# A score matrix made in two halves: second moments about the first 512 tokens' mean

## The reference, cut to what matters

```python
b, n, d = x.shape                       # x: 64 * 32 tokens, layer-normed, d = 256
q = jnp.einsum('bnd,de->bne', x, w_q)   # 2048 columns of w_q
mean = jnp.mean(q, axis=(0, 1))
var = jnp.var(q, axis=(0, 1))
q = (q - mean) * jax.lax.rsqrt(var + BN_EPS) * bn_gamma + bn_beta
q = q.reshape(b, n, 2, H, KD).transpose(2, 0, 1, 3, 4)
sim = jnp.einsum('pbnhd,hkpd->pbnhk', q, keys)        # 64 keys for each of 16 heads
...                                     # top 8 of 64, twice; top 8 of 64 sums; gather, gelu, weigh, sum
```

## Time and profile before

| | |
|---|---|
| median of 3 runs | 2900.16 us (2898.94 to 2902.98) |
| the profiled execution | 2904.19 us, span 2902.3 us |
| TensorE (PE) busy | 2571.6 us, 89% |
| VectorE (DVE) busy | 2047.8 us, 71% |
| ScalarE (ACT) busy | 1447.9 us, 50% |
| GpSimd (POOL) busy | 651.5 us, 22% |
| mean granted clock of TensorE | 0.948 |

### The profile page before, as it was taken

The page is one execution under the profiler, slowest core; times in us unless marked ns, Lnnn a source line. Parts: engine busy times, 40 slices in busy tenths (PEclk is TensorE's granted clock), DMA queues, the critical chain, the costliest instruction groups (busy, mean ns, idle before and its releaser), DMA issues. The chain is left out here.

```text
span 2902.3 us, 79978 instructions
## 1 busy us (share of the span) xinstructions
PE 2571.6 (89%) x29950; PEld 1911.7 (66%) x29951; DVE 2047.8 (71%) x4847; ACT 1447.9 (50%) x3937; POOL 651.5 (22%) x928
## 2 busy tenths in 40 slices
PE   8899999799788999999989999978777777769995
PEld 4688887355567888888875666653433333669995
DVE  6688886577539888888866888865699999532223
ACT  4455543355215555555546888842776764013331
POOL 5555553111000000000001333310222221014442
PEclk9999999899989999999999999989799999769998
DMA  4322221000300000000001111113000001351113
GB/s 123 87 71 71 71 71 35 1 1 0 142 41 2 3 2 2 2 2 2 2 12 48 47 47 44 46 39 122 1 1 1 1 1 59 141 211 36 36 37 105
DMA packets 86969, 128.29 MB, mean 44 GB/s; under 512 B 22877, under 2 KB 67357, under 8 KB 82558
## 3 DMA queue, kind: packets, MB, share of 16 engines
q1 hardware_dynamic: 80782, 113.18, 12.4%
q0 software_dynamic: 3744, 10.23, 1.1%
q10 hardware_dynamic: 2256, 2.16, 0.2%
HBM read 105.67 MB, written 19.87 MB: 43 GB/s over the span
## 5 line engine op out<-in xcount | busy, mean ns | idle before, releaser
L1405 PE MATMUL s_ps<-s3e_xT,s_down 128*128 128x128 f32 x2048 | 253.9, 278 | 0.0
L1405 PEld LDWEIGHTS s_ps<-s3e_xT,s_down 128*128 128x128 f32 x2048 | 242.4, 192 | 13.9 <-issue 8.1
L1416 PE MATMUL s_ps<-s_up,s3e_gh 128*128 128x256 f32 x1024 | 242.6, 381 | 4.3 <-DVE s3e_gh L1574 2.2
L1416 PEld LDWEIGHTS s_ps<-s_up,s3e_gh 128*128 128x128 f32 x1024 | 186.2, 191 | 26.6 <-issue 3.3
L1464 ACT ACTIVATE s3e_gh<-s_ps 128x512 f32<-128x512 f32 x128 | 76.6, 599 | 234.0 <-PE s_ps L1416 211.7
L2868 ACT ACTIVATE s6e_hT<-s_ps,s_b 128x128 f32<-128x128 f32 x312 | 84.9, 383 | 187.1 <-PE s_ps L2841 187.1
L2507 DVE SCALAR_TENSOR_TENSOR s5c_fresh<-s_ps,s5c_state 128x1024 f32<-128x1024 f32 x124 | 151.3, 1220 | 11.3 <-PE s_ps L2461 4.5
L1450 ACT ACTIVATE s3e_apart<-s3e_number,s3e_picksT 128x128 f32<-128x128 f32 x512 | 156.1, 389 | 1.6
L1827 PE MATMUL s_ps<-s4a_wv,s4a_cT 128*128 128x256 f32 (+1 forms) x512 | 151.5, 404 | 1.1 <-PEq L1655 1.1
L1680 POOL MEMSET s4q_half<- 128x1 f32 x1 | 0.1, 99 | 675.2 <-POOLq L2987 675.2
L2841 PEld LDWEIGHTS s_ps<-s6e_xT,s6e_w 128*128 128x128 f32 x1248 | 147.0, 194 | 5.4 <-ACT s6e_xT L2872 3.5
(11 more groups left out here) (431 smaller groups left out, 6303.4 us busy)
## 6 DMA issues: line engine op xcount, KB each, us to landing
s4a_cT<-ctxR SPq DMA_DIRECT2D x64, 257.0 KB, 2.7
s_w<-p_w SPq DMA_DIRECT2D x16, 1024.0 KB, 14.0
s_bcx<-ctx SPq DMA_DIRECT2D x64, 192.0 KB, 2.6
s_bcT<-ctxT SPq DMA_DIRECT2D x64, 192.0 KB, 3.0
s_down<-p_down SPq DMA_DIRECT2D x1, 4096.0 KB, 22.6
s_up<-p_up SPq DMA_DIRECT2D x1, 4096.0 KB, 31.8
s_silu_z<-s5p_sz SPq DMA_DIRECT2D x4, 1024.0 KB, 4.5
s_skipped<-s_xi SPq DMA_DIRECT2D x4, 1024.0 KB, 3.9
```

The lines of the kernel that those rows point to most:

```text
L1405: mm = pe.matmul(banks[:, H_BANK + i % 2, tok(e)], lhsT=down[:, k, i * CH + e, :], rhs=xT[:, c.u, k, :], start=k == 0, stop=k == KT - 1)
L1416: mm = pe.matmul(banks[:, Y_BANK, 0:D], lhsT=gh[:, o.u, e, :], rhs=up[:, e, :], start=e == 0, stop=e == NE - 1)
```

## The change

Five things, all in phase 3; what is computed stays the same up to rounding.

1. The moments are taken about `near`, the mean of the first 512 tokens (one group of four tiles), and no more about the mean of all. Column 256 of `xc` holds ones, so the product of `xc` with itself also gives the sum about `near`; the spread gets two more columns, (mean - near) and near. Variance is then w'Cw less the square of w.(mean - near), and the mean of a column the sum of both. The sum over tiles 4 to 15 goes; groups 2 and 3 are normed only after groups 0 and 1 were moved.
2. Of the second moments the block (1, 0) is no longer computed: half k = 1 has only columns 128 to 256. ScalarE copies half 0, TensorE transposes its right block, VectorE copies that to its place (`corner_ready`).
3. The row power is taken for 4 columns first, then for 12.
4. The statistics of the columns go in two halves of 8 column blocks: `variance`, the power, `scaled_keys`, `shifted_keys`, the map, the offset. TensorE no longer waits before column 8.
5. `count`, `parity` and `number` are loaded in `score_map`, ahead of `down` and `up`, and `retrieve` waits for that semaphore.

Of the diff the added lines and what stands around them; the lines that they replace are in the listing above, at the lines named there.

```diff
--- before.py
+++ after.py
...
+    NG, HP = 4, 8
+        xc = sb("xc", [P, NT, D + 1])
+        near = sb("near", [P, D])
+        cov = sb("cov", [P, KT, D + 2])
+        means = sb("means", [P, PH, 2])
...
         @block.sync
         def _(sp):
             for dst, src in ((wq, "p3_wq"), (wqT, "p3_wqT"), (keys, "p3_keys"), (gb, "p3_gb")):
                 sp.dma_start(dst[:], I[src]).then_inc(loaded, 16)
+            for name in ("count", "parity", "number"):
+                sp.dma_start(tables[name][:], I[{"count": "count8", "parity": "parity", "number": "row_no"}[name]]).then_inc(tables["numbers_loaded"], 16)
             sp.dma_start(tables["down"][:], I["p3_down"]).then_inc(tables["down_loaded"], 16)
             sp.dma_start(tables["up"][:], I["p3_up"]).then_inc(tables["up_loaded"], 16)
 
         @block.gpsimd
         def _(pool):
+            pool.memset(n.half[:], -0.5)
             pool.memset(ones[:], 1.0)
+            pool.memset(xc[:, :, D:D + 1], 1.0).then_inc(set_up, 1)
             pool.wait_ge(set_up, 1)
             pool.wait_ge(stat_ready, 1)
+            for ts in (slice(0, NG), slice(NG, NT)):
+                pool.tensor_tensor(n.rstd[:, ts], n.var[:, ts], bc(n.half[:], P, ts.stop - ts.start), ALU.pow).then_inc(rstd_ready, 1)
+            for h in range(2):
+                hs = slice(h * HP, (h + 1) * HP)
+                pool.wait_ge(var_ready, h + 1)
+                pool.tensor_tensor(rstd[:, hs], var[:, hs], bc(n.half[:], P, HP), ALU.pow).then_inc(vr_ready, 1)
 
         @block.tensor
         def _(pe):
             pe.wait_ge(set_up, 1)
+            pe.wait_ge(xn_ready, 1)
+            for t in range(NG):
+                mm = pe.matmul(banks[:, 0, 0:D], lhsT=ones[:], rhs=xc[:, t, 0:D], start=t == 0, stop=t == NG - 1)
             mm.then_inc(summed, 1)
+            pe.wait_ge(near_ready, 1)
+            for k in range(KT):
+                mm = pe.transpose(banks[:, 3, tok(k)], near[:, tok(k)], g.ident[:])
+            mm.then_inc(near_tr, 1)
             for t in range(NT):
                 pe.wait_ge(xc_ready, t // NG + 1)
                 for k in range(KT):
+                    mm = pe.matmul(banks[:, 1 + k, k * P:D + 1], lhsT=xc[:, t, tok(k)], rhs=xc[:, t, k * P:D + 1], start=t == 0, stop=t == NT - 1)
+                    if t == NT - 1:
+                        mm.then_inc(cov_summed, 1)
+            pe.wait_ge(cov_ready, 1)
+            pe.transpose(banks[:, 4, 0:P], cov[:, 0, CORNER], g.ident[:]).then_inc(corner_tr, 1)
             pe.wait_ge(loaded, 64)
 
             for c in range(PH):
+                if c >= 8 and c % NG == 0:
+                    pe.wait_ge(means_read, c // NG - 1)
                 for k in range(KT):
+                    if c == 0 and k == 1:
+                        pe.wait_ge(cov_ready, 2)
+                        pe.wait_ge(corner_ready, 1)
+                    mm = pe.matmul(banks[:, c % 8, 0:D + 2], lhsT=wq[:, k, tok(c)], rhs=cov[:, k, :], start=k == 0, stop=k == KT - 1)
                 mm.then_inc(spread, 1)
+            for h in range(2):
+                hs = slice(h * HP, (h + 1) * HP)
+                pe.wait_ge(kg_ready, h + 1)
+                if h == 0:
+                    pe.wait_ge(means_read, 3)
+                for k in range(KT):
+                    for c in range(h * HP, (h + 1) * HP):
+                        mm = pe.matmul(banks[:, 2 * h + k, c % HP * NK:(c % HP + 1) * NK], lhsT=wqT[:, c, tok(k)], rhs=kg[:, c, :], start=True, stop=True)
                     mm.then_inc(mapped, 1)
+                pe.wait_ge(ks_ready, h + 1)
+                if h == 0:
+                    pe.wait_ge(means_read, 4)
+                pe.matmul(banks[:, 4 + h, :], lhsT=ones[:], rhs=ks[:, hs, :].rearrange("p c k -> p (c k)"), start=True, stop=True).then_inc(moved, 1)
 
         @block.scalar
         def _(act):
+            act.wait_ge(near_tr, 1)
+            act.activation(cov[:, :, D + 1:D + 2], banks[:, 3, 0:KT * P].rearrange("p (k q) -> p k q", k=KT)[:, :, 0:1], ACT.Copy)
             for k in range(KT):
+                act.wait_ge(cov_summed, k + 1)
+                act.activation(cov[:, k, k * P:D + 1], banks[:, 1 + k, k * P:D + 1], ACT.Copy, scale=1.0 / T).then_inc(cov_ready, 1)
+            for h in range(2):
+                hs = slice(h * C, (h + 1) * C)
+                for k in range(KT):
+                    act.wait_ge(mapped, KT * h + k + 1)
+                    act.activation(pairs[:, k, hs], banks[:, 2 * h + k, :], ACT.Copy)
+                act.wait_ge(moved, h + 1)
+                act.activation(offset[:, hs], banks[:, 4 + h, :], ACT.Copy).then_inc(map_ready, 1)
+            act.wait_ge(map_ready, 2)
 
         @block.vector
         def _(dve):
             link = Link(dve, dve_link)
+
+            def normed(i):
+                for t in range(i * NG, (i + 1) * NG):
+                    ins = n.apply(dve, xc[:, t, 0:D], X, t)
+                return ins
+
+            def moved_near(i):
+                ts = slice(i * NG, (i + 1) * NG)
+                dve.tensor_tensor(xc[:, ts, 0:D], xc[:, ts, 0:D], bc(near[:].unsqueeze(1), P, NG, D), ALU.subtract).then_inc(xc_ready, 1)
+
+            def variance(h):
+                hs = slice(h * HP, (h + 1) * HP)
+                dve.tensor_tensor(mq[:, hs], means[:, hs, 0], means[:, hs, 1], ALU.add)
+                link(dve.tensor_tensor(square[:, hs], means[:, hs, 0], means[:, hs, 0], ALU.mult))
+                link(dve.tensor_tensor(var[:, hs], var[:, hs], square[:, hs], ALU.subtract))
+                dve.tensor_scalar(var[:, hs], var[:, hs], 0.0, BN_EPS, ALU.max, ALU.add).then_inc(var_ready, 1)
+
+            def scaled_keys(h):
+                hs = slice(h * HP, (h + 1) * HP)
+                dve.wait_ge(vr_ready, h + 1)
+                link(dve.tensor_tensor(gain[:, hs], rstd[:, hs], gb[:, 0, hs], ALU.mult))
+                dve.tensor_tensor(kg[:, hs, :], keys[:, hs, :], bc(gain[:, hs].unsqueeze(2), P, HP, NK), ALU.mult).then_inc(kg_ready, 1)
+
+            def shifted_keys(h):
+                hs = slice(h * HP, (h + 1) * HP)
+                link(dve.tensor_tensor(shift[:, hs], mq[:, hs], gain[:, hs], ALU.mult))
+                link(dve.tensor_tensor(shift[:, hs], gb[:, 1, hs], shift[:, hs], ALU.subtract))
+                dve.tensor_tensor(ks[:, hs, :], keys[:, hs, :], bc(shift[:, hs].unsqueeze(2), P, HP, NK), ALU.mult).then_inc(ks_ready, 1)
+
             row_stats(dve, link, g.stats, n.mv, n.var, LN_EPS).then_inc(stat_ready, 1)
             dve.wait_ge(rstd_ready, 1)
+            normed(0).then_inc(xn_ready, 1)
+            dve.wait_ge(rstd_ready, 2)
+            normed(1).then_inc(xn_ready, 1)
             dve.wait_ge(summed, 1)
+            dve.tensor_scalar(near[:], banks[:, 0, 0:D], 1.0 / (NG * P), None, ALU.mult).then_inc(near_ready, 1)
+            dve.wait_ge(near_ready, 1)
+            dve.wait_ge(xn_ready, 2)
+            moved_near(0)
+            moved_near(1)
+            for i in range(2, NT // NG):
+                normed(i).then_inc(xn_ready, 1)
+                dve.wait_ge(xn_ready, i + 1)
+                moved_near(i)
+            dve.wait_ge(corner_tr, 1)
+            dve.tensor_copy(cov[:, 1, 0:P], banks[:, 4, 0:P]).then_inc(corner_ready, 1)
             dve.wait_ge(loaded, 64)
             for c in range(PH):
                 dve.wait_ge(spread, c + 1)
+                link(dve.tensor_tensor_reduce(scrap[:], banks[:, c % 8, 0:D], wqT[:, c, :], 1.0, 0.0, ALU.mult, ALU.add, var[:, c:c + 1]))
+                if c % NG == NG - 1:
+                    at = c % 8 - NG + 1
+                    dve.tensor_copy(means[:, c - NG + 1:c + 1, :], banks[:, at:at + NG, D:D + 2]).then_inc(means_read, 1)
+                if c == HP - 1:
+                    dve.wait_ge(means_read, 2)
+                    variance(0)
+                if c == HP + NG - 1:
+                    scaled_keys(0)
+            dve.wait_ge(means_read, 4)
+            variance(1)
+            shifted_keys(0)
+            scaled_keys(1)
+            shifted_keys(1)
...
+            act.wait_ge(tables["numbers_loaded"], 48)
...
+            dve.wait_ge(tables["numbers_loaded"], 48)
```

More of the change, by code:

```diff
@@ L1246, in _ @@
                     mm.then_inc(mapped, 1)
-            pe.wait_ge(ks_ready, 1)
-            for n in range(2):
-                mm = pe.matmul(banks[:, 4 + n, :], lhsT=ones[:], rhs=ks[:, 8 * n:8 * n + 8, :].rearrange("p c k -> p (c k)"), start=True, stop=True)
-            mm.then_inc(mapped, 1)
+                pe.wait_ge(ks_ready, h + 1)
+                if h == 0:
+                    pe.wait_ge(means_read, 4)
+                pe.matmul(banks[:, 4 + h, :], lhsT=ones[:], rhs=ks[:, hs, :].rearrange("p c k -> p (c k)"), start=True, stop=True).then_inc(moved, 1)
@@ L1268, in _ @@
             row_stats(dve, link, g.stats, n.mv, n.var, LN_EPS).then_inc(stat_ready, 1)
             dve.wait_ge(rstd_ready, 1)
-            for t in range(NT):
-                ins = n.apply(dve, xc[:, t, :], X, t)
```

(19 more changed lines are left out.)

67 lines of the change are left out of this document (10 added, 57 removed).

## The result

The changed kernel takes 2869.72 us, the median of 4 runs (2865.89 to 2873.27), and the kernel before 2901.57 beside it (2898.94 to 2904.59): ratio 0.9887, 95% interval 0.9875 to 0.9899. A second comparison gave 2868.97 against 2902.29, ratio 0.9882 (0.9867 to 0.9897). The forecast was 2871, between 2865 and 2880. The profiled execution took 2871.10 us with a span of 2869.3, 33.1 us under the one before (2904.19).

What follows compares the result with a forecast made beforehand. The prediction took TensorE, idle or at a low clock in the score map, as what bounds the stage. Eleven terms from 0 to 6.5 us sum to 29.6 us, off 2900.2: 2871 us, range 2865 to 2880.

Steps and rivals of the forecast that it cites:

- sum: Score map's token sum: 32 records become 8, at 0.43 us each at the low clock, saving 5.1 us.
- moments: Second moments: half the records narrowed to 129 columns, gain 3.3 us less 0.8 for a late clock: 2.5 us.
- moments to spread: Between moments and spread: `near` transposed earlier and a first-row copy half as wide save 0.3 us, bounds 0 and 0.8.
- spread and idle time: Spread without the stop at column 8 saves 1.3 us; halved statistics remove 5.9 of TensorE's 5.93 us idle behind it.
- maps, offsets, last copy: End of score map: maps at full clock save 6.5 us; offset products and a copy half as wide save 2.4.
- to the first tile: Retrieval's start: early table loads remove VectorE's wait on DMA, saving 2.75 us.
- entry: Retrieval's first transposes and scores: less idle time ahead keeps the clock higher, saving 1.0 us, bounds 0 and 2.1.
- rival of the low clock in the moments: Clock stays low through sum and moments, one more rise about 3 us late: 2874 us, chance 0.10.
- no map at the low clock: Denies the rival that the clock falls in the maps: 2876 us, or 2879 with the first map; chance 0.20.
- no wait of TensorE for VectorE: Denies the rival that VectorE, feeder in three places with margins 0.1 to 0.35 us, is the bound: 2873 us, chance 0.10.
- no long stretch at the low clock in the retrieval: Denies the slower rival: retrieval runs long at 1.2 GHz, 2906 us at 70 us of it; chance 0.02.
- the early constants do what they say: Denies the rival that early tables don't help and maps stay at 0.50: 2883 us, chance 0.03.

Runs made afterwards that it cites:

- e1: Kernel before, with five unused 512-column products in TensorE's idle time between the spread and the maps: 2891.16 us, ratio 0.9961.
- e3: Changed kernel with the columns' statistics in one piece as before, after column 15: 2886.79 us, ratio 0.9947.
- f4: Kernel before with only the three small constants loaded early, the retrieval's own loads gone: 2899.51 us against 2903.48, ratio 0.9984.
- e7: Changed kernel with the mean taken over all 16 tiles again, all normed before any is moved: 2873.64 us, ratio 0.9910.
- e4: Changed kernel with count, parity and number loaded by the retrieval's own block again: 2870.17 us, ratio 0.9888.
- e2: Changed kernel with every map product done three times, same result each time: 2884.27 us, ratio 0.9935.
- e5: Changed kernel with the row power taken for all 16 columns at once, as before: 2876.72 us, ratio 0.9909.
- e6: Changed kernel with both halves of the second moments computed whole, no corner transposed: 2875.09 us, ratio 0.9911.
- f1: Changed kernel unaltered, run again beside two variants on one chip: 2868.97 us.
- f3: Changed kernel with filler products in TensorE's idle times, plus five more ahead of the last phase's router: 2860.32 us, ratio 0.9848.

## Why the prediction was right, step by step

| step | forecast | before, after (us) | measured |
|---|---|---|---|
| start | 1.8 | 6.03, 4.15 | 1.9 |
| sum | 5.1 | 8.54, 3.75 | 4.8 |
| gap | 0 | 1.78, 1.77 | 0.0 |
| moments | 2.5 | 14.08, 10.77 | 3.3 |
| moments to spread | 0.3 | 1.06, 0.43 | 0.6 |
| spread and idle time | 1.3 + 5.9 | 21.16, 14.23 | 6.9 |
| maps, offsets, last copy | 6.5 + 2.4 | 18.46, 9.66 | 8.8 |
| to the first tile | 2.75 | 3.23, 0.47 | 2.8 |
| entry | 1.0 | 8.10, 7.55 | 0.5 |
| sum | 29.55 | | 29.7 |

The first tile was foretold at some 818 and came at 817.77, and the mechanism is the one that was told: the idle time and the low clock behind it went together, and `e1` and `e3` show it from both sides. That the sum is met to 0.1 us is partly luck, for its terms missed by up to 0.8 us in both directions. So is the time: the difference was forecast 2.3 us too small (31.85 measured against 29.55), and the base, 2900.2, was 1.4 below the 2901.57 measured beside the changed kernel.

*The sum.* A record cost 3.75/8 = 0.47 us at the low clock, where the working had 0.43. More than that hangs on which execution of the kernel before is read. Its 32 records took 8.54 us in the profile shown and 8.52 in `e1`, but 10.20 in `f4`, which changes nothing there and enters with the clock low as well:

```profile
779.52 10.20 PE L1225 MATMUL s_ps<-s3s_xc,s3s_ones 128*128 128x256 f32 x32 [7.85 <-DVE s3s_xc L170]
```

Against such an execution the step gains 6.4 us, as in `e7`.

*The moments.* The working gave 3.3 and charged 0.8 for a late clock. In both profiled executions of this kernel (10.77 and 10.78 us) the clock was up at their first record and the 3.3 came whole; in `e4` too (10.78). In `e2`, `e3`, `e5` and `e6`, whose sum is the same, it was not, and 1.6 to 2.0 us were lost. The charge was a mean of two cases, and so right for neither. This is the rival of the low clock in the moments: it came in four of the seven traces that reach them in this way, where it was given a chance of 0.10, and it cost less than the 3 us that were its price.

*The entry.* I counted half of the 2.1 us, for an idle time that shrinks from 4.7 to 2. The scores still took 3.48 for 3.78. But one trace does not settle this term either. The first scores of `e7` and of `e5`, and of `e1`, whose TensorE idles as long as before's (4.65 us):

```profile
823.95 1.98 PE L1434 MATMUL s_ps<-s_pairs,s3e_xT 128*128 128x512 f32 x4 [0.56 <-ACT s3e_xT L1517]
...
823.27 3.78 PE L1434 MATMUL s_ps<-s_pairs,s3e_xT 128*128 128x512 f32 x4 [0.56 <-ACT s3e_xT L1517]
...
838.42 3.43 PE L1388 MATMUL s_ps<-s_pairs,s3e_xT 128*128 128x512 f32 x4 [0.56 <-ACT s3e_xT L1471]
```

The idle time ahead of the transposes is 1.57 or 1.58 us in `after` (the changed kernel's first profile), `f1`, `e2`, `e3`, `e5`, `e6` and `e7` alike. From the first tile to the first hidden product `e2` and `e7` took 6.05 us at a clock of 1.00, `after`, `f1` and `e6` 7.5 to 7.6, `e3` 8.1, and `e5` 9.75 at 0.53. So the length of the idle time alone does not give its price.

*From the moments to the spread, and the spread.* The first gained 0.6 for 0.3 and the second, with the idle time, 6.9 for 7.2; it is one shift. VectorE reads the columns 0.87 us apart, as foretold, and TensorE sets that pace. But the spread starts 0.4 us behind the moments, and its second product then waits for the corner's copy, which ends at 793.90; that took most of the 0.3 back: the first column is read 1.48 us after the spread's start, where it was 1.27. The small operations of `variance(0)` and `scaled_keys(0)` put VectorE behind, as foretold, and it made it up. VectorE in the spread's end and behind it:

```profile
805.20 0.69 DVE L1310 TENSOR_TENSOR s3s_kg<-s3s_keys,s3s_gain 128x512 f32<-128x512 f32 x1
805.81 0.42 DVE L1338 CUSTOM_DVE_ANT_0 s3s_scrap<-s_ps,s3s_wqT 128x256 f32<-128x256 f32 x1
...
807.08 0.42 DVE L1338 CUSTOM_DVE_ANT_0 s3s_scrap<-s_ps,s3s_wqT 128x256 f32<-128x256 f32 x1 [0.37 <-PE s_ps L1254]
...
811.22 0.69 DVE L1310 TENSOR_TENSOR s3s_kg<-s3s_keys,s3s_gain 128x512 f32<-128x512 f32 x1
```

At 807.08 it waits for TensorE again. The keys of the first half are ready at 805.89 and TensorE comes at 807.64; those of the second at 811.91, and it comes at 812.07, with the 0.2 us to spare that were forecast.

What the stage's sum doesn't hold is the rest of the difference: 31.9 and 33.3 us by the medians of two sessions, 33.1 between the two profiled executions, against 29.7. In the trace 1.5 of it lies in the retrieval behind its first tiles (664.4 us from the first hidden product to the phase's end before, 662.9 after), but among the kernels with the old map it is 662.9 in `e1` and 664.7 in `f4`, so it does not go with the change. The fourth phase does. It took 429.8 us before, 433.1 in `e1` and 431.2 in `f4`, and 425.8 to 427.9 in the eleven traces with the changed map. The group of TensorE that idles, over 300 us of that phase, of before, `f4` and after (columns: line, engine, operation, tiles and count, busy us and mean ns, idle us before them):

```profile
L1866 PE MATMUL s_ps<-s4b_kT,s4b_qb 32*64 32x257 f32 x848 | 36.6, 400 | 4.1 <-ACT s4b_kT L1899 1.2
```

```profile
L1862 PE MATMUL s_ps<-s4b_kT,s4b_qb 32*64 32x257 f32 x848 | 36.6, 400 | 4.1 <-ACT s4b_kT L1895 1.1
```

```profile
L1915 PE MATMUL s_ps<-s4b_kT,s4b_qb 32*64 32x257 f32 x864 | 37.3, 400 | 1.0
```

The clock is 1.00 in all three. In the timeline every second round takes 5.80 us before, in `e1` and in `f4`, and 5.72 in the traces with the changed map; the rounds between take 5.59 in all (in `before` they start at 1705.13, 1710.72 and 1716.51, in `after` at 1700.75, 1706.47 and 1712.06). That is 0.08 us in some 38 pairs of rounds, about 3 us. The change touches no line of that phase, and the constants' new place does not cause it, by `f4`. What else of the change does, is open; no experiment separates it from the map. The forecast had left such a thing out. In the phases 4 to 6 together the three kernels with the old map spend 1381.9 to 1384.9 us and those with the new one 1378.8 to 1384.6 (`f3` left out), so it shows in the sum by some 2 us in the mean, and the ranges overlap. A second source is the sum over all tiles: where it takes 10.2 us in place of 8.5, the kernel before is up to 1.7 us slower than the trace shown says. How often it does, no run shows.

Of the rivals four fell: no map at the low clock (the trace after, and `e2`), no wait of TensorE for VectorE in the trace after beyond those that stood there before, no long stretch at the low clock in the retrieval (0.99 over its 662.9 us), and the early constants do what they say (`e4`, `f4`). The fifth, the low clock in the moments, came in some executions and not in the one profiled first.

## What to carry to other kernels

Price an idle time of TensorE by the wait and by the clock of what stands behind it: here 5.9 us of waiting cost 8.5 more, and cutting a chain of small operations in two halves, so that the first half feeds TensorE while the second is made, brought both back. Where the wait can't be removed, independent products in it bring back the second part alone. A saving under 3 us is sized by the trace of one part undone, not by four runs. And before such a trace is read, compare the same instructions in other executions: the clock may rise sooner or later within them, and the same work then has more than one length (8.5 and 10.2, 10.8 and 12.7, 2.0 and 3.8 us here).

## What was not expected of the hardware

Records of 64 columns did not raise a low clock in 13.7 us of uninterrupted work, yet held a full one through two stretches of 10.8 us (`e2`). In `f4` the clock rose only within the four 512-column records behind such a map, which took 3.06 us in place of 3.73. At 0.115 us each they cost as much as 128-column records (0.117), so their own columns are not what sets their price. Five products of 512 columns, 4.6 us of TensorE in an idle time of 5.9, kept the clock at 1.00 through and behind it. The 64-column rows bear on the Trainium skill, page TensorE: Matmul & The Clock Gate, Part 1, by which activity releases the low clock: the trace of before disagrees for such records, as the prediction said, and in `e3` they ran at 0.50 again, 0.22 us each.
